# A sorted mixture-of-experts stage: two groups of two batches become one group of three, and the fourth batch runs through all experts

## What is computed

```
x = x + ga * attention(layernorm(x) * (1 + ca) + sa)
h = layernorm(x) * (1 + cb) + sb
probs = sigmoid(h @ router.T + bias);  top_w, top_idx = top_k(probs, 8)
top_w = 2.5 * top_w / sum(top_w)            # combine[t, e] = top_w where e is chosen, else 0
h1 = silu(einsum('th,eih->eti', h, w_gate)) # 64 wide for each expert
routed = einsum('eti,ehi->th', h1 * combine.T[:, :, None], w_down)
shared = silu(h @ w_gate_shared.T) @ w_down_shared.T
x = x + gb * (routed + shared)
```

## Time and profile before

| | |
|---|---|
| three runs | 918.35 us median (916.75 to 920.73) |
| profiled execution | 924.12 us, span 922.3 us |
| busy in the span | PE 732.7, DVE 551.9, ACT 467.5, POOL 593.3 us |
| mean granted clock of PE | 0.912 |

### The profile page before, as it was taken

How to read it: one execution, slowest core, us unless ns; L and a number is a source line. 1 busy time by engine, 2 the same in 40 slices (tenths; PEclk the granted TensorE clock), 3 DMA queues, 4 the chain that set the end, 5 groups by cost and what they waited for, 6 DMA issues and landing times.

```text
span 922.3 us, 15860 instructions
## 1 busy us (share of the span) xinstructions
PE 732.7 (79%) x5132; PEld 519.6 (56%) x5132; DVE 551.9 (60%) x1404; ACT 467.5 (51%) x969; POOL 593.3 (64%) x482
## 2 busy tenths in 40 slices
PE   4799989999999999899989994999669688770000
PEld 2656656666666656565656553778558577660000
DVE  5867666766676776767776763556233556551343
ACT  3666656666766557776667841543245344330000
POOL 0588878897788777778656765612731777306774
PEclk9899999999999999999999996999799989895555
DMA  7876966657666564775665859989989999952121
GB/s 226 233 209 189 273 172 195 176 167 187 179 161 182 153 189 124 197 208 141 180 173 147 272 190 387 350 264 301 358 286 301 326 301 302 344 208 78 51 65 48
DMA packets 84324, 195.91 MB, mean 212 GB/s; under 512 B 13602, under 2 KB 35556, under 8 KB 80532
## 3 DMA queue, kind: packets, MB, share of 16 engines
q1 hardware_dynamic: 67988, 148.76, 54.8%
q10 hardware_dynamic: 8064, 29.36, 8.2%
q0 software_dynamic: 8192, 16.79, 6.0%
HBM read 104.09 MB, written 70.32 MB: 189 GB/s over the span
## 4 chain that ended last, share of the span: by engine, by line
PE 44%; issue 14%; DVE 11%; POOL 11%; ACT 7%; SPq 6%; DMA 5%; DVEq 0%; POOLq 0%; ACTq 0%
PE ps L611 9%; PE ps L598 9%; PE ps L561 4%; POOL stack L1272 4%; ACT prob L1021 4%; PE ps L587 4%; PE ps L589 3%; POOL sorted_rows L1226 3%; PE ps L909 3%; PE ps L887 3%; DVE prob L1391 3%; SPq L471 3%; PE ps L924 2%; PE ps L624 2%; SPq L472 2%
## 5 line engine op out<-in xcount | busy, mean ns | idle before, releaser
L1209 POOL TENSOR_SCALAR prob<-prob,rinv 128x512 f32<-128x512 f32 x215 | 336.7, 1576 | 115.2 <-DVE rinv L1409 113.1
L1021 ACT ACTIVATE prob<-prob,nmax 128x512 f32<-128x512 f32 x256 | 182.9, 715 | 149.8 <-DVE nmax L1391 149.0
L1226 POOL DMA_INDIRECT sorted_rows<-xn,dest x128 | 126.6, 989 | 83.1 <-issue 83.1
L334 DVE COPY PT<-ps 128x512 f32<-128x512 f32 x128 | 88.3, 690 | 135.3 <-PE ps L598 134.2
L1391 DVE CUSTOM_DVE_ANT_0 prob<-ps,strips 128x512 f32<-128x512 f32 x256 | 164.9, 681 | 1.7 <-PE ps L589 1.1
L598 PEld LDWEIGHTS ps<-ident,prob 128*128 128x128 f32 x1024 | 115.6, 142 | 76.7 <-POOL prob L1209 40.5
L598 PE MATMUL ps<-ident,prob 128*128 128x128 f32 x1024 | 137.8, 278 | 4.4 <-ACT PT L334 4.0
L611 PE MATMUL ps<-PT,v_sb 128*64 128x512 f32 x512 | 123.8, 605 | 5.0 <-ACT PT L334 4.9
L1272 POOL DMA_INDIRECT stack<-sorted_rows,dest x64 | 61.7, 964 | 86.0 <-DMA sorted_rows<-prob 67.2
L587 PE MATMUL ps<-stack 128*128 128x512 f32 x256 | 113.6, 444 | 3.4 <-DVE nmax L1391 2.7
L1817 DVE COPY v_sb<-ps 128x512 f32<-128x512 f32 x56 | 38.6, 690 | 114.6 <-PE ps L887 114.5
(11 more groups left out here) (225 smaller groups left out, 1123.9 us busy)
## 6 DMA issues: line engine op xcount, KB each, us to landing
stack<-qk SPq DMA_DIRECT2D x128, 256.0 KB
sorted_rows<-in_zero_rows SPq DMA_DIRECT2D x28, 1024.0 KB, 5.6
wT<-sorted_rows SPq DMA_DIRECT2D x56, 512.0 KB, 6.2
sorted_rows<-prob ACTq DMA_DIRECT2D x38, 512.0 KB
strips<-in_expert_rows SPq DMA_DIRECT2D x128, 96.0 KB
sorted_rows<-woT ACTq DMA_DIRECT2D x18, 512.0 KB
k_low<-qk SPq DMA_DIRECT2D x64, 128.0 KB
hT<-qk SPq DMA_DIRECT2D x64, 128.0 KB
```

Of the source, the lines that this page charges most:

```text
L334: return copy(dst[:, :, qt * P:(qt + 1) * P], ps[:, BANK_T + u % 2, :].rearrange("p (k s) -> p k s", s=P))
L1021: nc.scalar.activation(prob[:, u, :], prob[:, u, :], ACT.Exp, bias=nmax[:, u:u + 1], scale=-1.0, accum_out=rsum[:, u:u + 1]).then_inc(s_ex ...
L1209: nc.gpsimd.tensor_scalar(prob[:, u, :], prob[:, u, :], rinv[:, u:u + 1], None, ALU.mult).then_inc(s_prob, 1)
L1226: nc.gpsimd.indirect_dma_start(sorted_rows[g], bass.IndirectOffsetOnAxis(ap=dest[:, n, k:k + 1], axis=0), rows[:, n, :], None).then_inc(s_ ...
```

## The change

- Batches 0, 1 and 2 are sorted as one group with 160 + 96 blocks, 32 steps, 12 of them chosen; chosen weights have a ring of four. The zero fills become 16. The third batch needs the counts of two batches before it (count, sum_blocks, set_bases, place); the masks of a finished batch are added up once (sum_masks).
- SP's first block load waits for the scatter of all three batches.
- Batch 3 isn't sorted. DVE makes a table of its weights for all 160 experts (combine_all_experts), PE transposes it, and it goes to DRAM (comb_rows). For each pair of experts ("pair" p of 80) PE multiplies both gates at once, 128x128 by 128x512 (dense_gate), ACT takes SiLU, DVE multiplies by the two experts' weight rows, which SP has loaded spread over 64 partitions each (load_spread, weigh), and PE adds the down product into one PSUM bank (dense_down). 15 pairs lie beside the 32 steps, one in every second step; 65 follow behind the steps.
- The shared expert, the owners' search and batch 3's router run between the routing of batch 2 and the first step.
- POOL picks 12 tiles instead of 16, all behind the last step, into a ring of six; DVE adds ten of them between the weighings of pairs 26 to 76, the last two around the scaling of batch 3's sum.

Its core:

```diff
-GROUPS = (Group((0, 1)), Group((2, 3)))
+SORTED = 3
+BLOCKS = E + EXTRA
+CHOSEN = [4 + 5 * k // 2 for k in range(CHOSEN_STEPS)]
-NX, NCHOSEN, NY, NGATHER = 6, 2, 3, 8
+NX, NCHOSEN, NY, NGATHER = 6, 4, 3, 6
+PAIRS = E // 2
+BESIDE = 15
...
+            def load_spread(i):
+                if i >= NROWS:
+                    sp.wait_ge(s_dweigh, 2 * (i - NROWS) + 2)
+                for half in range(2):
+                    of = comb_rows[4 * i + half:4 * i + half + 1, :]
+                    src = bass.AP(of.tensor, of.offset, [[0, I], [2 * S, 2], [1, S]])
+                    sp.dma_start(spread[i % NROWS][half * I:(half + 1) * I, :, :], src).then_inc(s_spread[i % NROWS], 16)
...
+            sp.wait_ge(s_owner, 1)
+            sp.wait_ge(s_dest, SORTED)
+            for k in range(NCHOSEN):
+                load_chosen(k, range(STEP))
+            sp.wait_ge(s_scatter, 16 * TILES * TOPK)
             for s in range(NX):
                 load_blocks(s)
+            sp.wait_ge(s_cst, 32)
+            for i in range(NROWS):
+                load_spread(i)
...
+            def dense_gate(p):
+                nc.tensor.matmul(ps[:, bank, :], known_weights[k][:, j * 2 * I:(j + 1) * 2 * I], h2T[:, :],
+                                 start=True, stop=True, skip_group_check=True).then_inc(s_dgate, 1)
+            def dense_down(p):
+                pe.wait_ge(s_dweigh, p + 1)
+                nc.tensor.matmul(ps[:, SUM_BANK, :], known_weights[k][:, STEP * I + j * D:STEP * I + (j + 1) * D],
+                                 dense[p % NDENSE], start=False, stop=p == PAIRS - 1,
+                                 skip_group_check=True).then_inc(s_ddown, 1)
             def beside(s):
+                if s >= 2 and s % 2 == 0:
+                    p = s // 2 - 1
+                    if p >= 1:
+                        dense_down(p - 1)
+                    dense_gate(p)
...
+            for p in range(BESIDE, PAIRS):
+                dense_gate(p)
+                if p == BESIDE:
+                    dense_down(p - 1)
+                if p - DENSE_AHEAD >= BESIDE:
+                    dense_down(p - DENSE_AHEAD)
...
-            for g in range(len(GROUPS)):
-                pick(g)
+            for r in range(NY):
+                pool.wait_ge(s_y[r], 16 * len(range(r, NSTEPS, NY)))
+            for n in range(TILES):
+                if n >= NGATHER:
+                    pool.wait_ge(s_fin, n - NGATHER + 1)
...
+            for p in range(BESIDE, PAIRS):
+                weigh(p)
+                if p >= 26 and (p - 26) * 2 % 11 < 2:
+                    combine(next(picks))
+            combine(next(picks))
+            dve.wait_ge(s_ddown, PAIRS)
+            nc.vector.tensor_scalar(dense_y, ps[:, SUM_BANK, :], modT[:, 5, LAST:LAST + 1], None, ALU.mult).then_inc(s_dy, 1)
+            combine(next(picks))
+            dve.wait_ge(s_dytr, 1)
+            nc.vector.tensor_tensor(x_all[:, LAST, :], x_all[:, LAST, :], ps[:, XT[0], :], ALU.add).then_inc(s_dfin, 1)
```

More of the change, by code:

```diff
@@ L59, in worst_extra, with step_blocks @@
     return best[-1]
[L62 to L68, removed]
-GROUPS = (Group((0, 1)), Group((2, 3)))
[L72 to L86, removed]
-NX, NCHOSEN, NY, NGATHER = 6, 2, 3, 8
-KNOWN_STEPS = E // STEP
-LATE = range(14, 18)
+SORTED = 3
+LAST = B - 1
+TILES = QT * SORTED
+EXTRA = -(-worst_extra(S * SORTED) // STEP) * STEP
+BLOCKS = E + EXTRA
+KNOWN_STEPS, CHOSEN_STEPS = E // STEP, EXTRA // STEP
+NSTEPS = KNOWN_STEPS + CHOSEN_STEPS
+CHOSEN = [4 + 5 * k // 2 for k in range(CHOSEN_STEPS)]
+def step_blocks():
+    known, chosen = iter(range(0, E, STEP)), iter(range(E, BLOCKS, STEP))
+    return [(next(chosen), True) if s in CHOSEN else (next(known), False) for s in range(NSTEPS)]
+STEPS = step_blocks()
+NX, NCHOSEN, NY, NGATHER = 6, 4, 3, 6
+LATE = (0, 1, 2, 3, 14, 15, 16, 17)
 RANK_UNIT = 512
 XT, GATE, DOWN = (0, 1), (2, 3), 4
-SIDE = (6, 7)
 SCATTERS = QT * TOPK
+PAIRS = E // 2
+BESIDE = 15
+DENSE_BANK, SUM_BANK = 6, 7
+NROWS, NDENSE, DENSE_AHEAD = 4, 3, 2
+MODULATE_BANK, LOGIT_BANKS, COMB_BANKS = 6, (7, 6), (6, 7)
+SHARED_BANKS = (2, 3, 4)
+BEFORE_BANKS, OWNER_BANK = (4, 5), 5
 ON_POOL, ON_ACT, ON_DVE = 0, 1, 2
@@ L264, in adaln_block @@
[L264 to L271, removed]
+            prob[:, 0:2, :].rearrange("p u n -> p (u n)"), prob[:, 4:6, :].rearrange("p u n -> p (u n)"), woT_flat))
@@ L426, in _ @@
             sp.dma_start(erow[32:33, :], route_table[0:1, 128:288]).then_inc(ld["small"], 16)
-            fills = [(g, w) for g, group in enumerate(GROUPS) for w in range(0, group.width, NT)]
             def fill(n):
[L431 to L434, removed]
+                w = n * NT
+                if w < BLOCKS:
+                    sp.dma_start(block_rows[:, w:w + NT, :], zero_rows.rearrange(
+                        "p (w d) -> p w d", d=D)).then_inc(s_fill, 16)
             for b in range(B - 1):
@@ L522, in _ @@
+            store(SORTED - 1)
             sp.wait_ge(s_out, 16 * B)
@@ L1744, in pair @@
                     match_weights(before)
+                elif before >= 0 and n == 6:
+                    sum_masks(before)
                 add_bias(b, n, 6)
@@ L1812, in _ @@
             destinations(2)
+            compare_blocks()
+            copy_owners()
+            combine_all_experts()
+            for b in range(SORTED):
+                add_shared(b)
             def copy_transposed(s):
@@ L1841, in beside @@
             def beside(s):
-                if s == 1:
+                if s == 0:
                     sum_top(2)
```

650 lines of the change are left out of this document (344 added, 306 removed).

## The result

Over 20 runs of each, the changed kernel has a median of 910.43 us and the kernel before 920.48; the ratio is 0.9884 (95% interval 0.9862 to 0.9906). It is faster, by 1.2%, where 4% was forecast, and 910.43 lies above the range of 866 to 904.

What follows compares the result with a forecast made beforehand. Bounds: TensorE in attention, transfers and TensorE together in the steps (265 us), GpSimd issuing in the last 92 us. Start +45.5, steps -126.2, behind them +42.2 make -38.5: span 884, median 880, range 866 to 904 (8 in 10).

Steps and rivals of the forecast that it cites:

- Routing, scatter, first step: Before the expert steps: batch 2's destinations end at 563.5, 32 scatter pieces follow, and the first step starts at 610.7.
- the 139: Expert stage: the 32 steps take 139 us instead of 265.2, as TensorE's and the transfers' bounds lie close together.
- TensorE's 131 us: Expert steps: TensorE's bound for 32 steps and 15 dense pairs, with half clock at the start; as a rival, chance 0.10.
- the bytes' 134 to 140: Expert steps: the transfers' bound, 127 us of DMA time taken at a share between 0.91 and 0.95.
- transfers pace the steps: Rival for the expert steps: transfers pace them as now, 152 us, total 893; chance 0.17.
- the rival with chance 0.04: Rival for the picks: VectorE operations with two SBUF inputs hold GpSimd off, adding 67 us, total 947; chance 0.04.
- 95 x 1.25 = 118.8: Picks behind the steps: 96 picks, each 1.25 us after the one before, 118.8 us from first to last start.
- The dense pairs: Behind the steps: 65 pairs at 1.78 us on TensorE, 115.7 us, plus 8 us of overruns behind ten tiles.
- the rival of the slower dense chain: Rival for the dense pairs: slower products, and half clock after each tile's overrun; end 25 us later, median 905; chance 0.12.
- 123.7: Dense pairs: time from the last step's end to the end of the last down product, at 873.4.
- last step to first pick: Seam behind the expert steps: the first pick starts 4.24 us after the last step's end, at 753.9.
- three signs of being wrong: Forecast wrong if the steps take over 150 us, a pair over 2.0, or a pick over 1.4.

Runs made afterwards that it cites:

- e1: Changed kernel, with ScalarE leaving SiLU of a dense pair's gate in PSUM and VectorE weighing it from there; median 902.01 us, ratio to before 0.9783.
- e2: Changed kernel, with the 64 loads of chosen experts' weights among the steps issued by GpSimd instead of SyncE; median 893.94 us, ratio to before 0.9667.
- e3: Changed kernel with both edits, those of e1 and e2; median 887.49 us, ratio to before 0.9612.
- e5: e3 with a combined tile's eight products made by ScalarE, all tiles but the last, VectorE's sum and additions split over two weighings; median 876.39 us, ratio 0.9508.
- e6: Changed kernel, with chosen loads taking constant experts, so SyncE reads no owner's number before issuing; one run, 892.81 us.
- e7: Changed kernel, with no dense pair beside the steps, all 80 behind, and spread loads beyond the first four behind too; one run, 898.15 us.
- e4: Kernel before, with seven extra VectorE operations behind each of six last-stage tiles: two SBUF inputs, one input in PSUM, or copies; span 922.0 us.

## Why the prediction failed

**Routing, scatter, first step: right.** 563.2 for 563.5, a scatter without gaps, 611.59 for 610.7: the seam is right. That the numbers agree to a microsecond is luck: in e1, e2, e3, e5, e6 and e7, which leave the routing as it is, the destinations come 2 to 6 us earlier and the first step is at 605.9 to 609.7.

**The steps: the transfers' side was the wrong resource.** The step that failed is the 139, taken from two sides only: TensorE's 131 us and the bytes' 134 to 140. As bounds both were near: with SyncE relieved the steps take 133.9 to 136.1 (e2, e3, e5, e6), TensorE without a gap and the DMA share at 0.93 to 0.98 from 650 to 740 us. SyncE's own time was put at nothing: the 64 chosen loads among the steps were counted in bytes alone, although the price of issuing one stood in the earlier trace rows (8.34 us for eight) and I used it myself for the 32 loads ahead of the steps. Counted from SyncE, 640.22 to 743.25 holds 62 of them x 1.04, 10 spread issues x 0.65 and 19 block loads x 0.55, together 81.5, and the gap behind each block load before the next chosen load, about 1.0, makes 101 of the 103.0 us. The rival "transfers pace the steps" had nearly the time (152), by the wrong cause: it spoke of spread rows, and e2 moves all the same bytes.

**The picks: the rival with chance 0.04 was the mechanism.** VectorE does hold GpSimd's picks. I priced it at every operation's whole length (67 us) and set it aside on the earlier trace rows, where a product begins at 895.84 and the pick at 895.82: that pick was 20 ns ahead, and a pick that has begun is not held. Seven of the eight products of that stage start within 50 ns of a pick, since each product is released by the tile's last pick and tiles are eight picks long, 10.0 us against 10.0; three of them start 20 to 30 ns ahead of the pick, and even there the pick lasts 0.94 or 0.95 and the product 1.27 to 1.28 instead of 1.22. So none of these picks begins well inside a product: the row was not evidence but a rhythm. Elsewhere the same trace had the answer, beside the second group's steps:

```profile
759.06 1.22 DVE L1832 TENSOR_TENSOR strips<-stack,wts 128x1024 f32<-128x1024 f32 x1
759.11 1.99 POOL L1272 DMA_INDIRECT qk<-sorted_rows,dest  x1 [0.30 <-issue]
```

The price is smaller than 67 because only a pick that starts inside such an operation waits, and only for its rest: 14.1. The second step that failed is "95 x 1.25 = 118.8"; e5 measures 119.0 once nothing holds. The Trainium skill, page "SBUF — State Buffer", section "Who interferes with whom", has the rule that a VectorE instruction with two SBUF inputs contends with a GpSimd instruction that reads SBUF. By e1 and e4 it is so here. I took its inference that building descriptors is spared as if the whole pick were; a pick that begins inside a product is not spared, 2.00 us against 0.95. Whether it waits with the read of its row numbers or with the building of descriptors no run separates; that a pick begun 20 ns ahead runs its 0.94 us beside the product unhindered speaks for its first moments.

**The dense pairs: sizes off, both ways, and no effect.** A pair takes 1.716 us, not 1.78. The ten stalls behind a tile are 13.6 us, not 8, and behind two of them, of 2.35 and 2.42 us, the granted clock is 0.50 to 0.57 for about three products, 3.4 us together: in part the rival of the slower dense chain. Its end, 132.3 us behind the steps, was forecast at 123.7; but the picks ended later, so nothing of it shows in the total. Whether it would once the picks are mended no run shows apart: e5 mends the picks and splits the tile's work at once.

**The whole.** Steps 9.9, picks 14.1, last step to first pick 1.5 (4.3 to 4.5 in every run of the changed kernel with an edit, near the forecast; why 5.7 here stays open), start 0.9, end 0.5: 26.9. The span fell 12.6 where 38.5 was forecast. None of the three signs of being wrong shows it: 148.9 us of steps against 150, 1.716 a pair against 2.0, and a pick every 1.399 us in the mean against 1.4, so the signs on steps and picks each allowed for their own miss, and the two together leave the range. With both causes taken out, e5 lies 45.8 us below before (922.19 on its chip), more than the forecast.

## What to carry to other kernels

Count three prices for a queue of transfers: its bytes, what waits in it, and the issuing engine's own time for each, above all where an address is read first; a queue that hardly ever waits (here 4.3 of 110 us) is a suspect, and relieving it is the test. Where a rival is dismissed on one row, look whether the two events in it are locked in step, and search the whole trace for a longer instance of the same operation (a 1.99 among 0.94). Beside GpSimd's indirect DMAs, give VectorE's products one operand in PSUM, or give them to ScalarE.

## What the runs showed of the hardware

A sum (128x1024, one SBUF input, 1.9 us) lengthened no pick: in the changed kernel none that began inside one lasted over 0.95 us. Copies of about 0.5 us from SBUF to SBUF added 0.1 at most. A held pick ends about 0.82 us after VectorE's operation. Near the operation's start the outcome varies: a pick 20 ns ahead of a product lasted 0.94, one 40 ns behind 2.00 (805.43), but another 40 ns behind 0.95 (827.46).

Idle time of the same length did not always lower TensorE's clock: behind the 2.42 us that ended at 877.02 the granted clock averaged 0.55 from 878.2 to 881.0, behind the 2.42 us that ended at 844.97 it was 1.00 from 845 to 848.

GpSimd issued a plain load of 96 KB with its address read from SBUF every 1.2 us (0.55 of it busy), about as fast as SyncE with 1.03 to 1.09.
